# Attention scores of two heads on separate 32-row groups of TensorE, in a ring of two-bank PSUM tiles

## What is computed

```python
x = x + 0.5 * ffn(layernorm(x))
x = x + attention(layernorm(x))
x = x + 0.5 * ffn(layernorm(x))

def attention(x):                       # 16 heads of 8 features
    q, k, v = heads of x @ q_w + q_b, x @ kv_w + kv_b
    att = q @ k.T / sqrt(8) + slope[h] * (key - query)     # slope = (h + 1) / 16
    att = where(key <= query, att, -inf)                   # causal
    return (softmax(att) @ v, heads joined) @ o_w + o_b
```

## Time and profile before

| | |
|---|---|
| time, median of 3 runs | 984.13 us (983.14 to 985.84) |
| profiled execution: span from the first to the last instruction | 984.3 us |
| first feed-forward layer, with set-up | 0 to 319 us |
| first max pass, alone | 326 to 361 us |
| attention, both passes | 366 to 744 us, about 50 us a batch in batches 1 to 5 |
| second feed-forward layer | 750 to 984 us |
| busy share of the span | PE 93%, DVE 68%, ACT 48%, POOL 15% |
| mean granted TensorE clock | 0.985 |

### The profile page before, as it was taken

How to read it: one execution, slowest core, us unless ns; L and a number is a source line. 1 busy time by engine, 2 the same in 40 slices (tenths; PEclk the granted TensorE clock), 3 DMA queues, 4 the chain that set the end, 5 groups by cost and what they waited for, 6 DMA issues and landing times.

```text
span 984.3 us, 19699 instructions
## 1 busy us (share of the span) xinstructions
PE 911.0 (93%) x6633; PEld 716.6 (73%) x6633; DVE 671.7 (68%) x2328; ACT 470.6 (48%) x791; POOL 147.9 (15%) x127
## 2 busy tenths in 40 slices
PE   1588999999999589999999999999998999999996
PEld 0477999999998456565656565656556999899996
DVE  1686677887775887676767575857424677788865
ACT  6221444454444116556555555555665444445442
POOL 2212022222210301100001010100003122222201
PEclk9999999999999789999999999999999999999998
DMA  8100000000000220202020202020000000000000
GB/s 250 45 2 1 1 1 2 0 0 0 0 1 19 50 49 21 61 11 60 11 58 13 56 14 55 16 53 20 3 1 2 1 12 12 12 11 5 7 12 21
DMA packets 19609, 23.88 MB, mean 24 GB/s; under 512 B 4136, under 2 KB 11088, under 8 KB 19280
## 3 DMA queue, kind: packets, MB, share of 16 engines
q1 hardware_dynamic: 17536, 20.55, 8.8%
q10 hardware_dynamic: 1872, 2.43, 0.8%
q0 software_dynamic: 128, 0.02, 0.0%
HBM read 7.26 MB, written 2.10 MB: 10 GB/s over the span
## 4 chain that ended last, share of the span: by engine, by line
PE 86%; DVE 10%; issue 2%; DMA 1%; ACT 1%; POOL 0%; DVEq 0%; SPq 0%; ACTq 0%
PE bank L1437 23%; PE bank L1565 9%; PE bank L1519 8%; PE bank L1589 8%; PE bank L1276 6%; PE bank L1277 6%; PE bank L1278 6%; PE bank L1496 3%; PE bank L1493 2%; PE pair L1276 2%; DVE arena L894 2%; PE bank L1499 1%; PE pair L1277 1%; PE pair L1278 1%; PE pair L1614 1%
## 5 line engine op out<-in xcount | busy, mean ns | idle before, releaser
L691 ACT ACTIVATE arena<-bank,b_sb 128x512 f32<-128x512 f32 x256 | 169.7, 687 | 213.5 <-PE bank L1278 212.4
L747 ACT ACTIVATE arena<-bank 128x512 f32<-128x512 f32 x320 | 187.1, 599 | 155.0 <-PE bank L1496 99.8
L1437 PEld LDWEIGHTS bank<-w_rot,arena 128*128 128x128 f32 x2048 | 244.6, 192 | 8.4
L1437 PE MATMUL bank<-w_rot,arena 128*128 128x128 f32 x2048 | 247.3, 275 | 0.0
L1061 DVE SCALAR_TENSOR_TENSOR arena<-bank,w_exp,arena 128x128 f32<-128x128 f32 x512 | 143.9, 344 | 96.1 <-PE bank L1437 96.0
L1519 PE MATMUL bank<-kZ,qT 128*128 128x512 f32 (+3 forms) x512 | 153.9, 373 | 10.9 <-DMA kZ<-oT 7.5
L1565 PE MATMUL bank<-qT,kZ 128*128 128x512 f32 (+3 forms) x512 | 157.5, 376 | 1.2 <-DMA qT<-mT_zero 1.2
L1519 PEld LDWEIGHTS bank<-kZ,qT 128*128 128x128 f32 x512 | 87.1, 200 | 52.1 <-issue 24.8
L1174 DVE TENSOR_REDUCE mx<-bank 128x1 f32<-128x512 f32 x128 | 87.9, 686 | 50.8 <-PE bank L1493 50.1
L1276 PE MATMUL bank<-parts,w_hi 128*128 128x512 f32 x256 | 111.2, 434 | 1.2 <-DVEq L917 1.2
L1277 PE MATMUL bank<-parts,w_hi 128*128 128x512 f32 x256 | 101.2, 395 | 0.0
(11 more groups left out here) (188 smaller groups left out, 1235.0 us busy)
## 6 DMA issues: line engine op xcount, KB each, us to landing
qT<-parts SPq DMA_DIRECT2D x42, 128.0 KB
kZ<-parts SPq DMA_DIRECT2D x168, 32.0 KB
out<-x_all SPq DMA_DIRECT2D x8, 256.0 KB, 2.3
arena<-in_bias_k ACTq DMA_DIRECT2D x1, 1024.0 KB, 5.4
arena<-in_bias_q ACTq DMA_DIRECT2D x1, 1024.0 KB, 8.2
arena<-in_ew SPq DMA_DIRECT2D x1, 1024.0 KB, 9.1
qT<-oT SPq DMA_DIRECT2D x6, 128.0 KB
kZ<-oT SPq DMA_DIRECT2D x24, 32.0 KB
```

The costliest lines, as they stand in the source:

```text
L691: nc.scalar.activation(hT[e % 2][:, j, :], ps_up[j][:, :], ACT.Gelu, bias=b1_sb[:, e, j:j + 1]).then_inc(hidden_ok.sem, 1)
L747: nc.scalar.activation(dst, src, ACT.Exp).then_inc(exp_ok.sem, 1)
L1437: last = mm(tile(ps_dn[e % 2], t), hT[e % 2][:, j, t * P:(t + 1) * P], w2_rot[:, e, j, :], start=(j == 0), stop=(j == NJ - 1))
```

## The change

- **Operands.** Each head gets 32 rows: 24 rows of parts, 3 of bias, 2 for the maxima. The four heads of a group lie at partitions 0, 32, 64 and 96 of `qT` and of the new `kT` (which has 4 x 512 columns instead of 16 x 512, and no zeros). A score matmul contracts 27 rows in the max pass and 29 in the exp pass.
- **Jobs.** Two heads are computed together, on neighbouring 32-row groups, into the two banks of one tile: 20 jobs ("full", "mixed", "both") for each batch and pass instead of 40 units. Each job issues its matmuls alternately for the two heads, then two mask matmuls over 128 rows. DVE reduces and ACT exponentiates both banks with one instruction of 1024 elements ("mixed" needs two in the max pass).
- **Ring.** Both passes share one ring of three two-bank tiles; max and exp jobs take turns. The max pass is four jobs further ahead. In the last batch the exp jobs use two of the tiles. `ps_m` has one bank in place of two.
- **Buffers.** Three operand buffers instead of two; separate SBUF tensors instead of shared ones; operands of a batch move in one piece with 24 DMAs (8 rows each), the maxima with 4 DMAs instead of 1.
- **Moved work.** `q_k_low` and the normalisation for attention move from DVE to POOL. For batch 0, `q_k_low` stands in POOL's program behind `difference` of the last chunk and `obias(0)`. Value products of two of the four key blocks follow each other without a score job between. The loop over batches is unrolled. ACT's copy of the third value group of the last batch comes after its last exponential, and the second feed-forward layer's first up-projection waits for `x_attended` of the last batch.

```diff
-BLOCK = NQ * HD
-ROW_MAX = 3 * BLOCK
-ROW_BIAS = ROW_MAX + 2 * NQ
+ROWS = 32
+ROW_BIAS = 3 * HD
+ROW_MAX = ROW_BIAS + 3
+K_MAX, K_EXP = ROW_MAX, ROW_MAX + 2
...
-AT_OUT, AT_NORMALISE = (5, 7, 9, 11), (6, 8, 10, 12)
...
-AT_VALUES = (2, 4, 5, 7)
-AT_MAX_T, AT_MAX = 36, 37
+BUFS = 3
+AT_X_T, AT_Q, AT_K, AT_V = 0, 2, 4, 5
+AT_OUT, AT_Y_T, AT_O_PROJECT = (7, 8, 9, 10), 11, 13
+AT_ADD, AT_STATS = 14, 15
+AT_MAX = 15
+AT_VALUES = ((7, 8, 8, 9), (11, 12, 12, 13), (17, 18, 18, 19), (1, 2, 2, 3))
+AT_O_EVAC = (10, 14, 0, 4)
+PAIRS = [(kind, 2 * half + odd, q) for half in range(2)
+         for kind, odd in (("full", 0), ("mixed", 0), ("both", 0), ("full", 1), ("mixed", 1)) for q in (0, 2)]
+A_AHEAD = 4
+JOBS = list(jobs())
+RING = {job: i % 2 if job[:2] == ("exp", BATCH - 1) else i % 3 for i, job in enumerate(JOBS)}
...
+        ring = [bank(f"ring{i}", (P, 2, 512)) for i in range(3)]
+        ps_o, ps_m = pair[:, 0, :], pair[:, 1, :]
...
+            def operands(b):
+                if b < BUFS:
+                    sp.wait_ge(bias_in, 2 * BUFS)
+                else:
+                    wait(sp, b_scores, b - BUFS)
                 wait(sp, qk_split, b)
+                for q in range(NQ):
+                    for r in range(3):
+                        row = ROWS * q + HD * r
+                        sp.dma_start(qT[b % BUFS][row:row + HD, :, :].bitcast(FP32),
+                                     qs[ROWS * q:ROWS * (q + 1), Q_PARTS[r], :].bitcast(FP32)).then_inc(operands_in.sem, 16)
+                        sp.dma_start(kT[b % BUFS][row:row + HD, :, :].bitcast(FP32),
+                                     ks[ROWS * q:ROWS * (q + 1), K_PARTS[r], :].bitcast(FP32)).then_inc(operands_in.sem, 16)
+            def maxima(b):
                 wait(sp, max_rows, b)
+                for q in range(NQ):
+                    row = ROWS * q + ROW_MAX
+                    sp.dma_start(qT[b % BUFS][row:row + 2, :, :].bitcast(FP32),
+                                 mT[2 * NG * q:2 * NG * (q + 1), :].bitcast(FP32)).then_inc(max_in.sem, 16)
+            operands(0)
+            operands(1)
+            maxima(0)
...
+            def attention_norm(b):
+                wait(pool, att_roots_ok, b)
...
+                nc.gpsimd.tensor_tensor(xh[:, :, :], xs(b), mv[:, :, 0:1].to_broadcast([P, NT, D]),
+                                        ALU.subtract).then_inc(xh_ok.sem, 1)
...
+                nc.gpsimd.tensor_tensor(xh[:, :, :], xh[:, :, :],
+                                        rstd[:, 0, :].unsqueeze(2).to_broadcast([P, NT, D]),
+                                        ALU.mult).then_inc(xh_ok.sem, 1)
...
             obias(0)
+            q_k_low(0)
+            v_place(0)
             attention_roots(1)
+            attention_norm(1)
             obias(1)
+            q_k_low(1)
...
+                            if at_turn(g) and e == 0:
                                 wait(pe, exp_ok, BATCH - 1)
+                                wait(pe, o_out, BATCH - 1)
+                                wait(pe, x_attended, BATCH - 1)
...
+                def heads(b, t, q, rows_):
+                    at = slice(ROWS * q, ROWS * q + rows_)
+                    return qT[b % BUFS][at, t, :], kT[b % BUFS][at, t, :]
+                def scores_for_max(b, m):
+                    kind, t, q0, two = scores_of(("max", b, m))
+                    if m == 0:
+                        wait(pe, operands_in, b)
+                    free_tile(("max", b, m))
+                    part = [heads(b, t, q0 + i, K_MAX) for i in range(2)]
                     if kind == "full":
+                        for i, (q_, k_) in enumerate(part):
+                            mm(two[:, i, :], q_[:, 3 * P:4 * P], k_, start=True, stop=False)
+                        for i in range(2):
+                            last = mm(two[:, i, 3 * P:4 * P], ident_bf[:, :], mask_qk[:, 0, :], start=False, stop=True)
                     elif kind == "mixed":
+                        for i, (q_, k_) in enumerate(part):
+                            mm(two[:, i, 0:3 * P], q_[:, 2 * P:3 * P], k_[:, 0:3 * P], ...)
+                        for i, (q_, k_) in enumerate(part):
+                            mm(two[:, i, 3 * P:4 * P], q_[:, 0:P], k_[:, 0:P], ...)
+                        for i in range(2):
+                            last = mm(two[:, i, 2 * P:4 * P], ident_bf[:, :], mask_qk[:, :, :]..., ...)
...
+                for m in range(A_AHEAD):
+                    scores_for_max(1, m)
+                    if m == 1:
+                        transpose_max(0)
```

More of the change, by code:

```diff
@@ L246, in macaron_block @@
         shrink = sb("shrink", [P, NROT, SQUARINGS])
+        ring = [bank(f"ring{i}", (P, 2, 512)) for i in range(3)]
         pair = bank("pair", (P, 2, 512))
-        banks = [bank(f"bank{i}") for i in range(6)] + [pair[:, 0, :], pair[:, 1, :]]
+        banks = [two[:, i, :] for two in (*ring, pair) for i in range(2)]
         ps_up, ps_dn = banks[0:2], banks[2:4]
@@ L357, in over_chunks, with evacuated, scores_of @@
             body(CH - 1, 1, False, True)
-        def over_batches(engine, body):
-            body(0, 0, True, 2)
-            with engine.Fori(0, (BATCH - 4) // 2) as i:
-                body(2 * i + 1, 1, False, 2)
-                body(2 * i + 2, 0, False, 2)
-            for b in range(BATCH - 3, BATCH):
-                body(b, b % 2, False, min(2, BATCH - 1 - b))
+        def evacuated(engine, job):
+            if job is not None:
+                kind, b, m = job
+                wait(engine, reduced if kind == "max" else exp_ok, b, m + 1)
+        def scores_of(job):
+            kind, t, q = PAIRS[job[2]]
+            return kind, t, q, ring[RING[job]]
         def xs(b, t=None):
@@ new lines, in maxima @@
+            def maxima(b):
+                wait(sp, max_rows, b)
+                for q in range(NQ):
[5 more added lines that the diff above has]
+            maxima(0)
+            for b in range(BATCH):
+                if b + 2 < BATCH:
+                    operands(b + 2)
+                if b + 1 < BATCH:
+                    maxima(b + 1)
@@ L977, in norms @@
                 wait(dve, roots_ok, g)
-                if isinstance(g, int) and g == CH:
-                    wait(dve, y_transposed, BATCH - 2)
-                elif not early(g, 0):
+                if not early(g, 0):
                     wait(dve, z_transposed, g - 1)
@@ L987, in split_ @@
                 wait(dve, xn_ok, g)
-                if isinstance(g, int) and g == CH:
-                    for half in operands_in:
-                        wait(dve, half, BATCH - 1)
-                elif not early(g, 1):
+                if not early(g, 1):
                     wait(dve, up_ok, g - 2)
@@ L1368, in project_v @@
-            def project_v(b):
-                wait(pe, q_out, b)
-                for t in range(NT):
-                    last = split_product(tile(ps_m[1], t), tile(x_hi, t), tile(x_lo, t),
+                    last = split_product(tile(bank_, t), tile(x_hi, t), tile(x_lo, t),
                                          small_hi[:, W_V:W_V + D], small_lo[:, W_V:W_V + D])
@@ L1502, in scores_for_max, with free_tile @@
[L1502 to L1512 removed]
+                def free_tile(job):
+                    before = job_before(job)
+                    if before is not None:
+                        evacuated(pe, before)
```

764 lines of the change are left out of this document (343 added, 421 removed).

## The result

The changed kernel takes 1122.72 us, median of four runs (1114.11 to 1126.8), against 983.63 before (982.87 to 985.84): 1.140 times as long, with an interval of [1.135, 1.145]. The forecast was 1030 us and the range ended at 1080: the side was right, the size far off. The profiled execution has a span of 1125.0 us and a mean granted clock of 0.851; before these were 984.3 and 0.985.

What follows compares the result with a forecast made beforehand. PE alone was taken to set the pace, busy 49.85 of 50.0 us in a steady batch. 984.3 + 31 (seven batches) + 16 (turn into attention) + 3 (end) = 1034, put at 1030 us; range 960 to 1080.

Steps and rivals of the forecast that it cites:

- The term for a steady batch: PE's score jobs in a batch: 31.9 us against 29.0, +2.9; with value blocks and maxima's wait, +4.4 a batch.
- Score jobs: PE per job: full 0.71, mixed 0.87, both 0.82 us; heads overlap fully, each job pays two changes between 32 and 128 rows.
- rivals 1 and 2: Two row groups' weight loads go in turn: 1072 us, chance 0.15; the pair's matmuls run in turn: 1090, chance 0.07.
- rivals 3 and 4: Changes of rows are cheap: 980 us, chance 0.16; weight loads also hide behind the other group's matmuls: 955, chance 0.09.
- rival 3: Cheap row changes in score jobs, 80 a batch: 980 us, chance 0.16; decides once a job averages under about 0.62 us.
- Maxima: At the turn between batches PE waits 2.1 to 2.9 us for the maxima's copy and four DMAs, +2.5 a batch.
- 2 us or more at each batch's start: Sign that the forecast is right: PE waits this long for the maxima's DMA.
- steady batches of 53 to 55 us: Sign that the forecast is right; a batch under 49 us would mean cheap row changes.
- Value blocks: Two value blocks of each group follow each other, saving 4 x 0.24 = 1.0 us of PE a batch.
- The turn into attention: Start of attention: late q and k splits on POOL and 24 DMAs delay PE; +16 us, bounds +8 and +22.
- The end: After the last exponential: copy 0.6, normalisations in series 3 x 0.5, up-projection waiting 0.7; +3 us.
- Batch 7's exp pass: Last batch, only exp jobs: +1.5 - 1.0, about 0.

Runs made afterwards that it cites:

- x4: x1 with each head's score matmuls contracting 64 rows, overlap and mode changes kept; scores not the reference's: 1006.78 us.
- x1: The changed kernel with 23 of the 24 operand DMAs of a batch left out; output is not attention's: 1074.66 us.
- x3: The changed kernel with the eight operand rows of each DMA three apart instead of neighbouring, same result: 1098.13 us, 1.117 times before.
- x2: x1 with every score matmul contracting all 128 rows, so no row groups, overlap or mode changes; scores not the reference's: 1004.11 us.
- x7: The kernel before with value blocks 0 and 1, and 2 and 3, following each other, seven merges a batch: 987.12 us, 1.0033 times before.
- x10: x3 with every mask matmul issued twice and batch 0's low halves of q and k back on DVE: 1063.7 us, 1.086 times before.
- x5: x1 with both heads of a pair on the same row group, so no overlap; scores not the reference's: 1255.42 us.
- x8: x3 with every mask matmul issued twice, same result: 1069.44, 1072.54 and 1079.81 us, 1.092 times before; a fourth run of 1787.63 us not counted.

## Why the prediction was right or wrong, step by step

**The step that failed: the clock as a constant.** The term for a steady batch, 31.9 us of scores against 29.0, took every cost at 2.4 GHz, because a steady batch of before has 1.00. The text even allowed that the low clock "may add some" in the first pass, and dropped it for the rest. The change brought matmuls over 27 to 29 rows, and with them the clock in the batches goes to and fro between 0.50 and 1.00, with a mean of 0.70 in 530 to 600 us. Per batch the excess over before is 13.0 us. x4, where the jobs are the same but for the rows (64 instead of 27 to 29), has an excess of 2.4 and x1, at 27 to 29 rows, of 10.4. So 8.0 us of it, 56 in seven batches, come from the rows in use; both are single runs, but 56 us is several times their spread. The 2.6 from the changed kernel to x1 are no more than two profiles may differ by, and x3 took the operand waits away without shortening the batches. Neither a term nor a rival of mine held a clock below 1.00 in the batches. Without these 56 us the result would have been near 1067, inside the range; without the miss of the turn alone, some 21 us, it would still have been outside.

**Score jobs: right within 9% at 2.4 GHz.** 0.65, 0.80 and 0.76 against 0.71, 0.87 and 0.82 us, all below by 0.06 or 0.07: the last score matmul to the mask's start costs 0.10 beside its columns, where I had 0.13 and 0.04, and the way back, about 0.10, is near the 0.11 I took. By the measured values the scores of a batch take 16 x 0.65 + 16 x 0.80 + 8 x 0.76 = 29.3 us, +0.3 rather than +2.9. The overlap of two heads, the heart of the change, does what it says: rivals 1 and 2 fall, and so do rivals 3 and 4, since a job costs 29.3 / 40 = 0.73 us on average, where rival 3 needed less than 0.62.

**Maxima: the wait is there, but smaller.** PE waits 12.5 us in 8, 1.6 each, at most 3.1, where 2.1 to 2.9 were forecast. x2 and x4 have the same (12.4 in 8 and 12.2 in 8). My sign "2 us or more at each batch's start" failed, as did the steady batches of 53 to 55 us.

**Value blocks: too large, and perhaps worth nothing.** I took 0.24 us a merge, four a batch, -1.0 us. In the kernel before seven merges brought 1.1 us of PE's time (x7), 0.16 each, and all of it was taken back by waits; the whole came out 0.3% slower. What the four merges do in the changed kernel was not tried alone. Work removed from a bound engine is time only if what feeds it is as far ahead.

**The turn into attention: right dependency, wrong size.** I had POOL's queue, the issue of 24 DMAs and then "lands about 2.3 after its issue, at 342". The last issue came at 341.29, and the landing took 11.37 us: PE began at 352.70. With rows three apart it began at 341.93, which is my 342 by luck: the first issue came at 322.9 where I had 325.2, and 24 issues 0.71 apart took longer than my 15.1 us. For the 2.3 no row stood beside it, and none of before showed a DMA that writes eight neighbouring rows. The first exp job stands at 403.87 instead of 381. Of the way to the first maxima DMA at 399.9, 9 us are the slow landing again for batch 1. Part is the clock, which I allowed for in words and put at nothing: from the first score matmul to the maxima DMA x1 takes 35.8 us at 0.50 and x4 31.8 at 0.66.

**The end: under-sized.** From the last value products to the first up-projection there are 8.5 us before (741.82 to 750.29) and 13.2 after (876.70 to 889.94), +4.8 for the forecast +3. PE stands idle 0.67 to 0.71 us before each step, and the clock is 0.81 in 875 to 891 where it was 1.00 in 738 to 752 before; the output projection takes 2.07 us, and 1.16 before. PE's timeline of the kernel before, then of the changed one:

```profile
741.82 2.34 PE L1589 MATMUL bank<-arena,vA 128*9 128x512 f32 x32 [1.30 <-ACT arena L747]
...
749.37 1.16 PE L1626 MATMUL pair<-wo_sb,work 128*128 128x128 f32 x8 [0.69 <-ACT work L772]
750.29 0.48 PE L1276 MATMUL bank<-parts,w_hi 128*128 128x512 f32 x1
```

```profile
876.70 2.34 PE L1585 MATMUL pair<-arena,vA 128*9 128x512 f32 x32 [1.36 <-ACT oT L777]
...
886.88 2.07 PE L1616 MATMUL pair<-wo_sb,yT 128*128 128x128 f32 x8 [0.69 <-ACT yT L783]
889.94 0.77 PE L1256 MATMUL ring<-parts,w_hi 128*128 128x512 f32 x1 [0.99 <-DVE x_all L1202]
```

Batch 7's exp pass, put at "about 0", grew from 37.5 to 44.0 us (from its maxima DMA to the last value products). x2 and x4 have most of this stage's excess at a clock near 1 (+9.3 and +8.9), so most of it does not come from the rows; order and waits are left, and were not separated further.

**The rest, by difference.** In x2 and x4 the batches still exceed those of before by 1.8 and 2.4 us, close to the wait for the maxima, 1.6. So at the old clock the batches would have lost some 14 us in all. With 9 for the end (x2) and 6 (x10) to 37 (after) for the turn, that puts the change near 1013 to 1044 us: an estimate from these rows, with the forecast's 1030 in the middle. So the side was not luck, but 1030 would have been in part: the batches were put too high (+31 for 14), the turn and the end too low (+16 for up to 37, +3 for 9). No run held the clock up with everything else unchanged.

## What to carry to other kernels

Before a matmul is cut to fewer rows to run several side by side, look at the granted clock as part of its price, and treat a steady 1.00 before as a property of the work, not of the engine: here two heads on 27 to 29 rows each cost 56 us more than two on 64 rows with the same overlap. A move of operands over few neighbouring partitions needs its own landing time; do not take that of a wide transfer. A saving on the bound engine has to be tried alone, as with the value blocks, before it is counted.

## What was not expected of the hardware

- A TensorE that never pauses can be held at 1.2 GHz: 100.00 of 100.00 us busy at 0.66 (x5), 10.00 of 10.00 at 0.50 (after). The mean clock went with the rows in use: 0.779 with 27 to 29 rows on one group, 0.871 with two such groups, 0.943 with two of 64, 0.969 with 128, and 0.787 when the masks were narrowed too. The Trainium skill (TensorE: Matmul & The Clock Gate, Part 1) ties the clock to how busy TensorE has been, and by that a busy engine would be at full speed; these stretches were busy and were not, so the measurement decides. Whether it is rows, cells or power that counts, these runs do not tell.
- Useless full-array matmuls made a kernel faster: 640 more of them, some 60 us at 2.4 GHz by the estimate above, and 1098.1 us became 1072.5 (x8).
- Two row groups load weights at the same time: the loads of a job's two heads start 3 or 4 ns apart in the packed trace of the changed kernel, and last 0.18 us each at 2.4 GHz.
- Eight neighbouring rows as the target of a transfer between SBUF tensors took the queue twice the time of eight rows three apart (11.3% of 1125.0 us against 5.4% of 1107.2), and the last of a burst of 24 landed 11.37 us after its issue against 2.30.
